# Layer 3 of a four-layer network: expert weights kept in SBUF and picked by register, 64-slot parts on the first 64 partitions, and shared products and layer ends in another order

## What is computed

```python
logits = jax.nn.log_sigmoid(x @ gate_weight.T)
probs = jax.nn.softmax(logits, axis=-1)
topw, topi = jax.lax.top_k(probs, TOP_K)          # two of 16 experts
...
w_up = _dequant(fc_up_qweights, fc_up_blocks_scale, fc_up_global_scale)
w_down = _dequant(fc_down_qweights, fc_down_blocks_scale, fc_down_global_scale)
z = jnp.einsum('th,ehi->tei', x, w_up)
a = jnp.square(jnp.maximum(z, 0.0))
aw = a * wdense[:, :, None]
y = jnp.einsum('tei,eih->th', aw, w_down)
```

## Time and profile before

| | |
|---|---|
| median of three executions | 630.23 us |
| profiled execution, its own time | 632.02 us |
| span of its instructions | 630.20 us |
| PE busy, share of the span | 502.8 us, 80% |
| DVE busy | 395.4 us, 63% |
| POOL busy | 285.3 us, 45% |
| ACT busy | 218.2 us, 35% |
| chain that ended last | PE 68%, DVE 11%, issue 7%, DMA 5%, ACT 4% |
| layer 3's part weights (wR<-w) | 48 DMAs of 256 KB |

### The profile page before, as it was taken

How to read it: one execution, slowest core, us unless ns; L and a number is a source line. 1 busy time by engine, 2 the same in 40 slices (tenths; PEclk the granted TensorE clock), 3 DMA queues, 4 the chain that set the end, 5 groups by cost and what they waited for, 6 DMA issues and landing times.

```text
span 630.2 us, 9033 instructions
## 1 busy us (share of the span) xinstructions
PE 502.8 (80%) x2760; PEld 337.1 (53%) x2760; DVE 395.4 (63%) x805; ACT 218.2 (35%) x555; POOL 285.3 (45%) x259
## 2 busy tenths in 40 slices
PE   1867745899999998998888969898989961967754
PEld 1554533687878776455555454455656461433324
DVE  6887793999999996477672775577621765000003
ACT  2412142222222224145554340355444340333332
POOL 4105306979999720336653002366665003366540
PEclk9778756999999996999999978999999965577796
DMA  8400012999864301736664499365232413889825
GB/s 229 88 2 33 0 34 67 243 239 236 221 164 138 95 1 63 191 101 220 200 183 147 150 291 235 86 212 169 79 90 68 142 45 108 258 270 271 237 86 198
DMA packets 84928, 92.80 MB, mean 147 GB/s; under 512 B 8370, under 2 KB 64274, under 8 KB 84882
## 3 DMA queue, kind: packets, MB, share of 16 engines
q1 hardware_dynamic: 75858, 67.56, 37.7%
q0 software_dynamic: 9024, 24.65, 13.4%
HBM read 72.79 MB, written 19.40 MB: 146 GB/s over the span
## 4 chain that ended last, share of the span: by engine, by line
PE 68%; DVE 11%; issue 7%; DMA 5%; ACT 4%; another core or an unknown queue 2%; POOL 2%; DVEq 0%; SPq 0%; POOLq 0%; ACTq 0%
PE y_ps L647 9%; PE g_ps L777 7%; PE g_ps L741 5%; PE u_ps L741 5%; PE u_ps L620 5%; PE r_ps L724 4%; PE u_ps L693 4%; PE y_ps L530 4%; PE g_ps L702 3%; PE y_ps L711 3%; PE g_ps L782 2%; PE r_ps L762 2%; PE g_ps L635 2%; DMA xg<-ctab,idx 2%
## 5 line engine op out<-in xcount | busy, mean ns | idle before, releaser
L1734 POOL DMA_INDIRECT xs<-ctab,idx_g x76 | 75.6, 995 | 141.2 <-DVE idx_g L1371 70.4
L1741 POOL DMA_INDIRECT ybuf<-o_s,idx_s x76 | 76.3, 1004 | 89.1 <-ACT o_s L964 70.6
L1702 POOL DMA_INDIRECT xg<-ctab,idx x36 | 54.5, 1514 | 36.3 <-DVE idx L1514 28.8
L647 PE MATMUL y_ps<-P,o_hi 128*128 128x512 f32 x144 | 59.7, 414 | 0.2 <-DVE o_lo L1539 0.2
L724 PE MATMUL r_ps<-ident_s,xs 128*128 128x128 f32 x152 | 34.3, 311 | 29.7 <-ACT hT_s L957 13.8
L647 PE MATMUL y_ps<-P,o_lo 128*128 128x512 f32 x144 | 56.6, 393 | 0.0
L1395 DVE TENSOR_TENSOR h_s<-a_s 128x128 f32<-128x128 f32 x24 | 7.1, 297 | 69.8 <-ACT a_s L950 33.6
L724 PEld LDWEIGHTS r_ps<-ident_s,xs 128*128 128x128 f32 x152 | 18.5, 152 | 54.7 <-issue 44.8
L964 ACT ACTIVATE o_s<-g_ps 128x256 f32<-128x256 f32 x76 | 29.1, 383 | 48.8 <-PE g_ps L777 22.9
L942 ACT ACTIVATE xT_s<-r_ps 128x256 f32<-128x256 f32 x76 | 28.8, 379 | 38.3 <-PE r_ps L724 34.6
L620 PE MATMUL u_ps<-xT_g,wup 128*96 128x96 f32 x384 | 37.8, 253 | 0.7 <-DVE hT L1533 0.7
(11 more groups left out here) (265 smaller groups left out, 1112.7 us busy)
## 6 DMA issues: line engine op xcount, KB each, us to landing
wR<-w SPq DMA_DIRECT2D x48, 256.0 KB
wup<-in_wglu SPq DMA_DIRECT2D x36, 256.0 KB
ysb<-ybuf SPq DMA_DIRECT2D x6, 1024.0 KB, 6.7
wR<-in_wglu SPq DMA_DIRECT2D x4, 1216.0 KB
wdn<-in_wglu SPq DMA_DIRECT2D x12, 384.0 KB
raw_q<-in_wq SPq DMA_DIRECT2D x16, 256.0 KB
w<-w3o SPq DMA_DIRECT2D x16, 256.0 KB
ctab<-ysb SPq DMA_DIRECT2D x6, 512.0 KB, 3.1
```

The source lines that it names most:

```text
L647: mm = pe.matmul(y_ps[:, m, hf, :], o[:, b, m * P:(m + 1) * P], P1[:, b, hf * HALF:(hf + 1) * HALF], start=first and n == 0, stop=last and ...
L1702: pool.indirect_dma_start(out=xg[:, j % XG, :], out_offset=None, in_=ctab, in_offset=bass.IndirectOffsetOnAxis(ap=idx[:, j:j + 1], axis=0) ...
L1734: pool.indirect_dma_start(out=xs[:, n % XB, :], out_offset=None, in_=ctab, in_offset=bass.IndirectOffsetOnAxis(ap=idx_g[:, b:b + 1], axis= ...
L1741: pool.indirect_dma_start(out=ybuf, out_offset=bass.IndirectOffsetOnAxis(ap=idx_s[:, b:b + 1], axis=0), in_=o_s[:, n % OB, :], in_offset=N ...
```

## The change

The weights of all 16 experts of layer 3 are loaded once into SBUF by four DMAs of 1 MB each, which SP issues after the row loads of layer 2's end (`load_w3`). PE reads two expert numbers per block into registers and addresses the weights by them. Both parts of a block now have their products on partitions 0 to 63, side by side in the free dimension: up in one bank, and down in two banks of `y_ps` in turn. `turn_h` becomes two transposes of 64 rows, and `block_out` two copies, which also multiply by the down scale; the up scale is applied in ACT's Relu. `scale_w3` is gone: DVE unpacks straight into the tile that is stored, and waits for that tile's earlier store. In the fronts of layers 1 and 2 the first gate product stands ahead of the positions, five of the six gate and up products ahead of the lists, and three banks and three buffers are used for them. At the ends the last shared down product stands between the two halves of `final`, and DVE and ACT weigh the rows by halves. A recurrence unit moves from layer 1's end into layer 2's blocks, which take 28 parts, and layer 1's 20. Line numbers behind the change are some 10 to 16 higher.

```diff
-Q0 = [0, UNITS + NGR, UNITS + NGR + 6]
-QN = [0, 6, 6]
+Q0 = [0, UNITS + NGR, UNITS + NGR + 5]
+QN = [0, 5, 7]
 DQ = [0, 10, 6]
...
 
-            def load_parts():
-                sp.wait_ge(be_ready, 3)
+            def load_w3():
                 for s in range(2):
                     sp.wait_ge(w3_in[s], 16 * E3 // 2)
-                for t in range(NP[3] * BK[3]):
-                    w = t % WB
-                    if t >= WB:
-                        sp.wait_ge(bd_done, B0[3] + (t - WB) // NP[3] + 1)
-                    e = sp.value_load(be[t:t + 1, 0:1], min_val=0, max_val=E3 - 1)
-                    sp.dma_start(w3r[:, w, :], w3[bass.ds(e, 1), :, :].rearrange("a p n -> p (a n)")
-                                 ).then_inc(w_in[w], 16)
+                for e in range(0, E3, 4):
+                    sp.dma_start(w3r[:, e:e + 4, :], w3[e:e + 4, :, :].rearrange("e p n -> p e n")
+                                 ).then_inc(part_in, 16)
...
                     load_up2()
+                if layer == 2:
+                    sp.wait_ge(bd_done, B0[3])
+                    load_w3()
...
                 j, hf = k // 2, k % 2
-                gk_, m, tok = NSH * (layer - 1) + k, SHW[k // 2], slice(hf * HALF, (hf + 1) * HALF)
+                n, m, tok = NSH * (layer - 1) + k, SHW[k // 2], slice(hf * HALF, (hf + 1) * HALF)
                 if k == 0:
                     pe.wait_ge(wsh_in, 16 * SHQ[layer])
-                    pe.wait_ge(ctok_ready, 4 * layer + 4)
-                if k == SHEAD:
+                    wait(pe, sha_ready, n)
+                elif k == 2:
+                    pe.wait_ge(sha_ready, n - 1)
+                elif k == SHEAD:
                     pe.wait_ge(bh_ready, B0[layer] + BK[layer])
...
                                    start=kt == 0, stop=kt == KT - 1, skip_group_check=True)
                 mm.then_inc(shg_done, 1)
 
             def shared_up(layer, k):
                 j, hf = k // 2, k % 2
-                gk_, m, tok = NSH * (layer - 1) + k, SHW[k // 2], slice(hf * HALF, (hf + 1) * HALF)
-                wait(pe, shh_ready, gk_)
+                n, m, tok = NSH * (layer - 1) + k, SHW[k // 2], slice(hf * HALF, (hf + 1) * HALF)
+                if k == 1:
+                    pe.wait_ge(ctok_ready, 4 * layer + 4)
+                elif k > SHEAD:
+                    pe.wait_ge(shh_ready, n)
                 for kt in range(KT):
...
-                    t = NP[3] * b
+                    if b == 0:
+                        pe.wait_ge(part_in, 16 * E3 // 4)
                     for g in range(NP[3]):
-                        pe.wait_ge(w_in[(t + g) % WB], 16 * ((t + g) // WB + 1))
-                    for kt in range(KT):
-                        for g in range(NP[3]):
-                            part = slice(g * GS[3], (g + 1) * GS[3])
-                            mm = pe.matmul(bank2(n)[part, 0:P], xT_s[:, s, kt, part],
-                                           w3r[:, (t + g) % WB, kt * P:(kt + 1) * P],
-                                           start=kt == 0, stop=kt == KT - 1, skip_group_check=True)
+                        own = w3r[:, bass.ds(e[g], 1), :].rearrange("p a n -> p (a n)")
+                        for kt in range(KT):
+                            mm = pe.matmul(bank2(n)[0:GS[3], g * P:(g + 1) * P], xT_s[:, s, kt, g * GS[3]:(g + 1) * GS[3]],
+                                           own[:, kt * P:(kt + 1) * P], start=kt == 0, stop=kt == KT - 1,
+                                           skip_group_check=True)
                 mm.then_inc(bu_done, 1)
...
-                    mm = pe.transpose(r_ps[:, KT * P:(KT + 1) * P], h_s[:, n % 2, 0:P], ident_s[:, :])
+                    m = GS[3]
+                    for g in range(NP[3]):
+                        mm = pe.transpose(r_ps[:, KT * P + g * m:KT * P + (g + 1) * m],
+                                          h_s[0:m, n % 2, g * P:(g + 1) * P], ident_s[0:m, 0:m])
...
-                wait(pe, o_ready, n)
+                wait(pe, o_ready, n if layer < 3 else n - 1)
...
-                        part = slice(g * GS[3], (g + 1) * GS[3])
-                        mm = pe.matmul(dst[part, :], hT_s[:, s, 0, part], w3r[:, (NP[3] * b + g) % WB, C:2 * C],
-                                       start=True, stop=True, skip_group_check=True)
+                        own = w3r[:, bass.ds(e[g], 1), :].rearrange("p a n -> p (a n)")
+                        mm = pe.matmul(y_ps[0:GS[3], 0, s, g * C:(g + 1) * C], hT_s[:, s, 0, g * GS[3]:(g + 1) * GS[3]],
+                                       own[:, C:2 * C], start=True, stop=True, skip_group_check=True)
...
+                if shared:
+                    shared_gate(layer, 0)
                 positions2(layer)
                 if shared:
-                    shared_gate(layer, 0)
                     shared_up(layer, 0)
                     shared_gate(layer, 1)
+                    shared_up(layer, 1)
+                    shared_gate(layer, 2)
                 lists2(layer)
                 if shared:
-                    shared_up(layer, 1)
-                    shared_down(layer, 0)
-                    shared_down(layer, 1)
-                    shared_gate(layer, 2)
                     shared_up(layer, 2)
-                    shared_down(layer, 2)
+                    for k in range(SHEAD):
+                        shared_down(layer, k)
...
+                final(layer, 0)
+                if shared:
                     shared_down(layer, NSH - 1)
-                for hf in range(2):
-                    final(layer, hf)
+                final(layer, 1)
...
+                                   ).then_inc(o_ready, 1)
+                else:
+                    m = GS[3]
+                    for g in range(NP[3]):
+                        ins = act.activation(o_s[g * m:(g + 1) * m, n % OB, :], y_ps[0:m, 0, n % 2, g * C:(g + 1) * C],
+                                             ACT.Copy, scale=gsc[0:m, 1:2])
+                    ins.then_inc(o_ready, 1)
...
-            def scale_w3(e):
-                act.wait_ge(deq_ready, e + 1)
-                wait(act, w3_in[e % 2], 16 * (e // 2))
-                for k in range(2):
-                    cols = slice(k * C, (k + 1) * C)
-                    ins = act.activation(w3o[:, e % 2, cols], raw_s[:, e % 2, cols], ACT.Copy,
-                                         scale=gsc[:, k:k + 1])
-                ins.then_inc(w3o_ready, 1)
...
-                    for k in range(SHEAD, NSH):
+                    for k in range(SHEAD, NSH - 1):
                         shared_silu(layer, k)
                 for i in range(TT):
+                    if shared and i == TH:
+                        shared_silu(layer, NSH - 1)
                     weigh_first(layer, i)
...
             def unpack(e):
                 s = e % 2
                 dve.wait_ge(q_in[s], 16 * (2 + KT) * (e // 2 + 1))
-                dve.scalar_tensor_tensor(out=raw_s[:, s, :], in0=raw_q[:, s, :], scalar=-8.0, in1=raw_s[:, s, :],
-                                         op0=ALU.add, op1=ALU.mult).then_inc(deq_ready, 1)
+                wait(dve, w3_in[s], 16 * (e // 2))
+                dve.scalar_tensor_tensor(out=w3o[:, s, :], in0=raw_q[:, s, :], scalar=-8.0, in1=raw_s[:, s, :],
+                                         op0=ALU.add, op1=ALU.mult).then_inc(w3o_ready, 1)
...
-                    if layer < 3 and b < 4 * (QN[layer] - 1):
+                    if layer < 3 and b < 4 * QN[layer]:
                         wkv_part(Q0[layer] + b // 4, b % 4)
                     e = unpacked(layer, b)
                     if e is not None:
                         unpack(e)
                 if shared:
-                    q = Q0[layer] + QN[layer] - 1
-                    for k in range(SHEAD, NSH):
+                    for k in range(SHEAD, NSH - 1):
                         shared_product(layer, k)
-                        for ph in range(2 * (k - SHEAD), min(2 * (k - SHEAD) + 2, 4)):
-                            wkv_part(q, ph)
-                for i in range(TT):
+                for i in range(TH):
                     weigh_second(layer, i)
-                for hf in range(2):
-                    add_y(layer, hf)
-                    if layer < NL - 1:
-                        cond(layer + 1, hf)
+                if shared:
+                    shared_product(layer, NSH - 1)
+                else:
+                    add_y(layer, 0)
+                for i in range(TH, TT):
+                    weigh_second(layer, i)
+                if shared:
+                    add_y(layer, 0)
+                    cond(layer + 1, 0)
+                add_y(layer, 1)
+                if shared:
+                    cond(layer + 1, 1)```

PE at the front of layer 2 (`sel` the choices, `wsu` the shared weights), before:

```order
L562 MATMUL g_ps<-ident_s,cnd 128x128 x16
L665 MATMUL r_ps<-sel,tri 128x112
L668 MATMUL r_ps<-sel,ones 128x112
L668 MATMUL r_ps<-sel,ones 128x98
```

74 lines of the change are left out of this document (41 added, 33 removed).

## The result

The changed kernel took 638.6 us at the median of four executions (636.5 to 645.0), the kernel before 630.2: ratio 1.0155 (95% interval 1.0106 to 1.0205). The forecast was 621, range 608 to 636. On a second chip, twelve executions of it and 23 of the kernel before had medians of 638.2 and 631.7, ratio 1.0024 (0.9977 to 1.0072). All ratios leave out executions more than 1.5% above a kernel's fastest, six of the twelve here (which span 628.7 to 650.3, against 626.0 to 636.1 for the kernel before), so these medians lie further apart than the ratio says. The gain of 9.2 us that was forecast, 1.5%, lies outside both intervals. A loss is clear in the first comparison, of four executions each; in the second the medians are 6.5 us apart, and the ratio can't be told from 1.

A forecast was written before the change was run, and what follows sets the result against it. PE was taken to bound layers 1 and 2, and layer 3 at the low clock. Terms -0.8 - 7 - 1.7 - 0.9 - 1 + 2.2 = -9.2 took 632.02 to 622.8, 621 at the median; range 608 to 636.

The forecast's parts named there:

- the gain per unpacking: Layers 1 and 2: removing ACT's scaling of unpacked weights saves 0.54 us per unpacking, 8.6 for 16.
- the gain from the filled fronts: Fronts: shared products placed in PE's waits give -0.8 us in layer 1 and, with the moved unit, -1.7 in layer 2.
- the cover over layer 3's products: Layer 3 at full clock: PE's block of 2.43 us stays hidden under POOL's gather and scatter pitch of 2.57.
- Eight in a row would be 0.90: Layer 3: up and down products lose their overlap and take 0.90 us each; block 2.43 us, bounds 1.83 to 3.03.
- The clock in layer 3: Layer 3's blocks: busier PE raises the clock sooner; low for about 14 us, three blocks at 4.65.
- the -7: Blocks of layers 1 and 2: removing the scaling from ACT gives -7 us, bounds -14 and -1.
- a pitch near 3.0: Sign in layer 1's blocks: pitch near 3.0 us, with PE's waits behind ACT shorter; wrong if it stays 3.24.
- Layer 3's end: End of layer 3: DVE's addition before weighing the second half delays the sums by +2.2 us, bounds 0 and +3.
- Layer 2's end: End of layer 2: the first half of the final sums comes 1.80 us earlier, half of it counts: -0.9 us.
- The moved unit: Layer 2's front: the recurrence unit taken from layer 1's end shares in a possible 4.5 us, counted as -1.7.
- The first rival: All blocks: ACT's stalls go with the ring's traffic, 6 us in layer 3, up to 10 in layers 1 and 2: 612; chance 0.14.
- a sign of traffic: Layer 3: ACT's unexplained waits fall from 8.3 to 5 us or less if traffic is part of them.

The follow-up runs named there:

- run 2: Changed kernel with constant expert numbers in layer 3, so no registers on PE and output of other experts: 644.7 us, ratio 1.0093.
- run 3: Changed kernel with constant experts in layer 3 (wrong output), no registers, and each part on its own half of the partitions: 637.1 us, ratio 0.9988.
- Run 8: Kernel before with only the scaling taken from ACT (scales applied late, DVE unpacks straight into the stored tile): 631.9 us, ratio 1.0013.
- run 5: The changed kernel itself, measured again on a second chip beside the kernel before: 638.2 us, ratio 1.0024.
- run 6: Changed kernel with PE's order in the fronts of layers 1 and 2 as before the change: 637.4 us, ratio 1.0100.
- run 10: Changed kernel with layer 3 as before, and three of layer 2's four large up loads ahead of the table's store: 634.7 us, ratio 1.0054.
- run 11: As run 10, with PE's fronts of layers 1 and 2 in the order from before the change: 630.2 us, ratio 0.9984.
- run 13: Layers 1 and 2 as in the changed kernel, layer 3 on the ring with up products that come out transposed: 637.6 us, ratio 1.0119.
- run 14: As run 13, with PE's order in the fronts of layers 1 and 2 as before the change: 634.2 us, ratio 1.0039.
- run 1: Changed kernel with DVE weighing all rows at layer 3's end before adding the first half to x: 643.5 us, ratio 1.0005.
- run 16: As run 14, with the last shared down product ahead of both halves of the final sums, as before the change: 632.8 us, ratio 1.0016.
- run 7: Changed kernel with the recurrence units as before the change, 20 parts in the blocks of layers 1 and 2 each: 638.4 us, ratio 1.0112.
- run 18: Kernel before without ACT's scaling, with moved unit, three banks, and layer 3's resident weights, registers and shared-partition products as changed: 640.0 us, ratio 0.9962.
- run 12: The kernel before, unchanged, measured once more against itself: 631.7 us, ratio 0.9965.
- run 15: As run 14, with the first gate product ahead of the positions, as in the change: 637.5 us, ratio 1.0023.

## Why the prediction was wrong, point by point

The first profiled execution came out 15.2 us over the 622.8 forecast for it: 9.2 in layers 1 and 2, 5.9 in layer 3 with its end. Three steps failed: the gain per unpacking, the gain from the filled fronts, and the cover over layer 3's products.

**Layer 3's products: the mechanism right, the size not, and the cover gone.** "Eight in a row would be 0.90" was taken from sums at 0.1125 each; they took 1.02, and the four down products 1.08, 0.13 per 128 columns, and 0.30 without a product came on top. That gave 3.0 in place of 2.43, inside the stated bounds. The step that failed is the next one: "at full clock 2.43 lies under POOL's 2.57, so the loss is hidden". The middle of the bounds was just under the cover and most of the upper half above it, so the term should have had the loss of uncovered blocks in it: fifteen at 3.0 instead of 2.57 are 6.5 us, and the last four 2.3. Runs 2 and 3 show the cause: the same products on two halves of the partitions take 0.66 and 0.65.

The sum's other parts missed too, in both directions. From the second turn (533.44) to the last (604.88), 22 intervals took 71.4 us, where 67.3 was forecast: the first three 8.7 in place of 14, as the clock rose sooner still; the next fifteen 50.7 in place of 38.6 and 5 of stalls; the last four 12.1 in place of 9.7. And the sum had no term for a clock that falls again. Before the change it fell several times in this stage (0.83 from 551 to 611, in place of 1.00), so a pitch near 3.1 there was in part PE at the low clock; in the changed kernel it fell once.

**The clock in layer 3: right in direction, too long in size.** The low stretch was to last about 14 us. It lasted 5 from the first up product at 534.03, which took 1.97; the turn at 539.38 and what follows are at full clock:

```profile
539.38 0.41 PE L734 MATMUL r_ps<-ident_s,xs 128*128 128x128 f32 x2 [0.46 <-ACT hT_s L976]
539.72 1.09 PE L759 MATMUL u_ps<-wR,xT_s 128*64 x8
```

Windows of the changed kernel, and of the kernel before, at the rise:

```profile
536.00:540.00 4.00, 3.54 (x17) 2.56 (x18) 0.84 (x2) 1.71 (x5) 0.95 (x1) 0.63 0.25 67
540.00:544.00 4.00, 3.93 (x27) 2.66 (x26) 0.42 (x1) 2.59 (x8) 0.41 (x1) 1.00 0.00 0
```

```profile
548.00:552.00 4.00, 4.00 (x28) 1.93 (x24) 0.55 (x2) 1.75 (x6) 2.14 (x3) 0.67 0.90 271
552.00:556.00 4.00, 1.82 (x19) 0.95 (x15) 0.15 (x1) 1.04 (x3) 3.08 (x4) 1.00 0.87 293
```

The second profile of the changed kernel has it at 544 (first up product at 539.2), that of the kernel before at about 549 (535.7). The reason given, that a busier PE comes with the full clock, is not borne out: in the earlier trace rows PE was as busy in the 17 us at 0.51 (14.74 of 17) as in layer 1 at 0.98 (66.46 of 76), and in run 3, with the short products and resident weights, the clock rose as soon (first up product at 542.5, full clock from 546.5). What brought the earlier rise stays open.

**Blocks of layers 1 and 2: the -7 failed.** Its step was "the pitch with unpackings is 3.24 and without 2.97, so 0.54 per unpacking". Run 8 took away just that and the time did not change. Three things were wrong with the step. The 3.24 came from one execution with stalls of ACT in it: by the same rows of the chain the second profile has 3.10 (and 84.5 us for those blocks), the changed kernel 3.02, so the sign "a pitch near 3.0" came true mostly by chance. The two pitches are of different layers and stretches. And the 0.71 behind a scaling is a wait of the weight load, not of PE's products, whose wait there was 0.18:

```profile
284.06 0.39 PE L762 MATMUL r_ps<-ident_s,h_s 128*88 128x128 f32 x2 [0.18 <-issue]
```

What layer 1's blocks did give (1.5 to 5.7 us by two profiles of each kernel) was taken back ahead of layer 2: its loads wait for the last shared down product (360.49 in the changed kernel, 360.63 before), the table waits for the loads, and the gather for the table.

**Fronts: the wrong sign.** That the table sets the first gather of layer 2 was forecast and happened. But the forecast counted the filled wait as a gain anyway (-1.7, and -0.8 in layer 1); it was +2.8 and +2.4 by the first gather, +0.5 and -0.1 by the first up product, and more behind it. Products that had stood between the lists and the first turn were moved ahead of the lists. In layer 1 they made the lists and so the first gather late: it came 13.0 to 14.1 us behind the start of the last turn of c in ten profiles with the changed order, 10.1 to 11.6 in nine with the old. In layer 2 they left 3.68 us with nothing to do and the low clock behind them: the first up product took 2.6 to 2.7 us in nine of those ten, 1.45 in all of those nine. "What stands ahead of the lists delays them" stood in the prediction, with no number.

Putting the old order back was worth 0.8, 4.5 and 3.4 us at the median in three pairs (runs 5 and 6, 10 and 11, 13 and 14), though by the ratio the first pair points the other way. The profiles of the three pairs agree. From PE's first up product to the last scatter, layer 1's blocks took 73.0, 76.2 and 72.9 us with the changed order and 71.1, 73.4 and 70.5 with the old; layer 2's took 93.1, 93.9 and 92.9 against 88.8, 88.6 and 88.2. Layer 2's first up product came only 0.9 to 1.2 us sooner for it. This is the largest loss that the runs tie to one edit in layers 1 and 2.

**Layer 3's end: right,** +2.2 forecast, +2.4 measured, 2.5 by run 1. **Layer 2's end:** -0.9 forecast; -0.7 between the layers in the first pair of profiles, but run 16, with the old order, lost nothing there (42.1 against 42.5), so the gain is not shown. **The moved unit:** nothing that the times show (run 7). **The first rival's sum** has -2.7 where the term for layer 2's front is -1.7, with no reason given; it would be 613 with it.

**What made the scatter larger is only partly shown.** ACT stalls at times with no releaser in the trace (the earlier trace rows has those of one of its instructions), in both kernels: 13 to 16 times in the blocks of an execution, up to 3.6 us, and 11 to 24 times, up to 4.65, over all the runs. A long one leaves PE dry, and the clock falls behind it. In the changed kernel, layer 3, timelines of ACT and PE:

```profile
559.18 0.47 ACT L968 ACTIVATE a_s<-g_ps,gsc 64x256 f32<-64x256 f32 x1 [3.57 <-remote]
...
559.96 0.66 PE L734 MATMUL r_ps<-ident_s,xs 128*128 128x128 f32 x2 [2.93 <-ACT hT_s L976]
560.55 1.97 PE L759 MATMUL u_ps<-wR,xT_s 128*64 x8
562.45 0.47 PE L776 MATMUL r_ps<-ident_s,h_s 64*128 64x64 f32 x2
562.85 1.97 PE L794 MATMUL y_ps<-wR,hT_s 128*64 x4
```

The stall costs 3 us, and the products after it 1.97 in place of 1.09 and 1.08. The granted clock in layer 2's blocks was 1.00 and 0.98 in the two profiles of the kernel before, 0.98 and 0.93 in those of the changed one, and between 0.90 and 1.00 over all kernels, with blocks of 96 to 108 us. Whether the change makes such dips more frequent, by taking away what kept PE busy behind ACT, was argued and not shown: over the kernels with the scaling gone and the changed front, layer 2's blocks took 98.9 to 107.8 us (ten profiles, mean 103.3), with the old front and eight more parts on DVE 97.8 to 105.9 (six, mean 100.5), ranges that overlap, on different chips. What the stalls are stays open too. In layer 3 they did fall in the changed kernel, from 12.9 and 15.9 us in the two profiles before to 3.6 and 2.1, under the 5 us that the prediction named as a sign of traffic. But they didn't go with the ring's traffic (12.2 us in run 3 and 10.6 in run 2, without it), which speaks against the first rival.

No version beat the kernel before clear of the interval. Of those with the right experts, the lowest median against it is that of run 11, by 1.1 us, ratio 0.9984 (0.9941 to 1.0026), and the lowest ratio that of run 18, 0.9962 (0.9899 to 1.0025), hardly under the 0.9965 of run 12, which is the kernel before itself.

## What to carry to other kernels

When a cost is called hidden, compare the cover with the upper bound of the cost, not with its middle: here 2.57 us of cover stood over a cost of 1.83 to 3.03. Here small products side by side on the same output partitions took 1.09 us, and on different halves 0.66; a resident table of weights that comes with the first placing has to earn that back. Work that fills a wait is taken from somewhere: look at what the engine has left to do at the next wait, and which clock it will be at behind it. Cut stages where the bounding engine begins its work, not where the first transfer is issued. And a pitch read from one execution holds its chance stalls; where a stage scatters by several us, take a second profile before it becomes a term.

## What the runs showed of the hardware that was not expected

- In four kernels (runs 13 to 16), whose up products in layer 3 had 64 columns, the granted clock was 0.50 for the whole stage of 86 us, with PE busy 41.0 of the last 43 in run 14. In the kernel before, with up products of 128 columns there, the clock rose after about 16 us of blocks, with PE busy 14.74 of 17.
- Eight products of 64 output rows and 128 columns: 0.66 us on two halves of the partitions, 1.09 on one, the same with and without a register instruction ahead of each.
- The same code of layer 1's blocks took 81.5 to 87.7 us in eight profiled executions, and 91.5 in a ninth.
- The kernel before had medians of 638.6 and 631.3 us on one chip, in two groups (35 executions each).
